# Pairwise tower on one core: the first twelve couples gathered one 128-sample block at a time, each four gathers followed by a wait for their landing, and product kinds read from a table

## What is computed

```python
e = jnp.stack([tbl_0[ids[:, 0]], ..., tbl_39[ids[:, 39]]], axis=1)      # 512 x 40 x 64
p, q = e[:, rowidx], e[:, colidx]                                       # all pairs i < j
z = jnp.einsum('bie,fie,bif->bi', p, param, q)                          # 512 x 780
h = jnp.concatenate([z, dense_ctx], axis=1)
h = jnp.maximum(h @ W_top1 + b_top1, 0.0)
h = jnp.maximum(h @ W_top2 + b_top2, 0.0)
y = h @ W_top3
```

## Time and profile before

| | |
|---|---|
| median of three runs | 346.36 us |
| lowest, highest | 344.58, 348.38 us |
| the profiled execution, its own time | 347.48 us |
| its span (first to last instruction) | 345.7 us |
| what lies around the span | 1.8 us |
| TensorE's granted clock, mean | 0.985 |
| busy: PE, DVE, ACT, GpSimd | 304.5, 260.8, 231.3, 217.4 us |

### The profile page before, as it was taken

One profiled execution on the slowest core, in us unless ns is written; L12 is line 12 of the kernel. 1 busy time (PEld: TensorE's weight loads), 2 busy tenths in 40 slices (PEclk: granted clock), 3 DMA queues, 4 the chain that ended last, 5 costly groups with the idle time before them and its releaser, 6 DMA issues.

```text
span 345.7 us, 7011 instructions
## 1 busy us (share of the span) xinstructions
PE 304.5 (88%) x2192; PEld 156.7 (45%) x2192; DVE 260.8 (75%) x278; ACT 231.3 (67%) x1783; POOL 217.4 (63%) x217
## 2 busy tenths in 40 slices
PE   0348837987999999999999999989999999999997
PEld 0123413443544444445654646554544534456665
DVE  0024773994999999999888697867789999986450
ACT  1000854675799779989835998893889988990003
POOL 5777777888688888888876867864686322220000
PEclk9999996998999999999999999999999999999999
DMA  3133584452444433411145453318433234000000
GB/s 78 27 77 94 147 288 147 150 144 94 126 139 141 154 95 95 156 33 35 25 121 139 133 159 99 123 47 322 143 126 123 58 123 149 2 1 3 0 2 0
DMA packets 12935, 35.57 MB, mean 103 GB/s; under 512 B 4705, under 2 KB 5985, under 8 KB 11618
## 3 DMA queue, kind: packets, MB, share of 16 engines
q1 hardware_dynamic: 7778, 29.88, 25.8%
q0 software_dynamic: 5120, 5.25, 7.5%
HBM read 35.12 MB, written 0.00 MB: 102 GB/s over the span
## 4 chain that ended last, share of the span: by engine, by line
PE 56%; issue 15%; DVE 14%; POOL 10%; ACT 3%; DMA 3%; DVEq 0%
PE upsum L596 18%; DVE prod L665 12%; PE upsum L591 11%; POOL emb L431 10%; PE zbank L546 9%; PE upsum L490 4%; PE abank L490 4%; PE abank L468 2%; ACT prod L703 2%; DMA emb<-tbl,rows_id 2%; PE upsum L558 2%; DVE z L639 2%; PE upsum L562 1%; PE abank L526 1%; PE upsum L615 1%
## 5 line engine op out<-in xcount | busy, mean ns | idle before, releaser
L703 ACT ACTIVATE prod<-prod 128x64 f32<-128x64 f32 x864 | 206.5, 243 | 7.2 <-DVE prod L665 6.5
L431 POOL DMA_INDIRECT emb<-tbl,rows_id x160 | 151.7, 948 | 52.0 <-issue 37.9
L703 ACT ACTIVATION_READ_ACCUMULATOR prod<-prod 128x1 f32 x864 | 163.7, 189 | 0.0
L665 DVE TENSOR_TENSOR prod<-upsum,emb 128x1024 f32<-128x1024 f32 x108 | 128.0, 1215 | 24.8 <-PE upsum L596 24.6
L596 PE MATMUL upsum<-w,xT 64*128 64x512 f32 x432 | 114.6, 630 | 3.6 <-DVE prod L665 2.6
L665 DVE TENSOR_TENSOR prod<-upsum,xT 128x1024 f32<-128x1024 f32 x72 | 85.7, 1215 | 24.2 <-PE upsum L591 24.1
L448 POOL TENSOR_TENSOR prod<-prod 128x512 f32<-128x512 f32 x51 | 65.0, 1277 | 38.8 <-DVE prod L665 38.2
L591 PE MATMUL upsum<-xT,w 64*128 64x256 f32 x576 | 78.4, 399 | 2.0 <-DVE prod L665 1.3
L591 PEld LDWEIGHTS upsum<-xT,w 64*128 64x128 f32 x576 | 54.8, 191 | 28.7 <-issue 13.6
L596 PEld LDWEIGHTS upsum<-w,xT 64*128 64x128 f32 x432 | 37.8, 189 | 48.0 <-issue 24.1
L546 PE MATMUL zbank<-prod,sel 128*32 128x256 f32 x696 | 50.8, 386 | 0.0
(11 more groups left out here) (42 smaller groups left out, 156.9 us busy)
## 6 DMA issues: line engine op xcount, KB each, us to landing
w<-W_top SPq DMA_DIRECT2D x2, 1792.0 KB, 9.4
emb<-tbl,rows_id POOLq DMA_INDIRECT x160, 2.5
w<-param SPq DMA_DIRECT2D x2, 1248.0 KB, 6.9
w<-param SPq DMA_DIRECT2D x2, 1152.0 KB, 5.0
w<-param SPq DMA_DIRECT2D x2, 1120.0 KB
w<-param SPq DMA_DIRECT2D x2, 1024.0 KB, 4.9
w<-param SPq DMA_DIRECT2D x2, 992.0 KB, 4.8
w<-param SPq DMA_DIRECT2D x2, 896.0 KB
```

The costliest lines, as they stand in the source:

```text
L431: pool.indirect_dma_start(emb[:, c, f, :], None, tables[f], bass.IndirectOffsetOnAxis(ap=rows_id[:, c, f:f + 1].bitcast(U32), axis=0),).th ...
L665: dve.tensor_tensor(to.rearrange("p (h q) -> p h q", h=2), t[:], f.broadcast_to([P, 2, BANK]), ALU.mult).then_inc(multiplied, 1)
L703: last = act.activation(ring[:, x * E:(x + 1) * E], ring[:, x * E:(x + 1) * E], ACT.Copy, accum_out=z_view(u)[:, x:x + 1])
```

## The change

The gathers of half 0's first twelve couples (0 to 11) are made block by block: first the 24 gathers of block 0, then the 24 of block 1. Ahead of every four of them but the first two fours, GpSimd waits until the four just issued have landed (a semaphore per couple for block 0, `first_gathered`). That makes ten waits. All later gathers keep their numbers: couple 12 at 16 and 18, couple 13 at 21 and 23.

The stretches of units get a part. Part 0: eleven units of block 0 of couples 4 to 11 come first, with a turn of block 0 alone ("xa", one transpose). Part 1: the other 25 units of couples 1 to 11, with the turn of block 1 ("xb"). Part 2 is the rest. The parameters of couples 4 to 11 are loaded twice, once for each part. The unit count stays 200, and unit 36 is still the first of couple 12.

The kinds are no longer made by shares but read from `KINDS`. Counted over both kernels:

| units | T | C | S | H | V |
|---|---|---|---|---|---|
| before, all 200 | 72 | 20 | 54 | 51 | 3 |
| after, all 200 | 72 | 20 | 52 | 34 | 22 |
| before, 0 to 29 | 9 | 5 | 8 | 5 | 3 |
| after, 0 to 29 | 6 | 5 | 6 | 0 | 13 |
| before, 36 to 99 | 24 | 4 | 18 | 18 | 0 |
| after, 36 to 99 | 30 | 4 | 17 | 13 | 0 |
| before, 100 to 199 | 36 | 10 | 27 | 27 | 0 |
| after, 100 to 199 | 34 | 10 | 27 | 20 | 9 |

```diff
-TURNS_BACK = [0, 0, 0, 0, 0, 0, 0, 0, 2, 2, 4, 4]
+TURNS_BACK = [1, 0, TURN_BACK]
-GATHER_FIRST, GATHER_FROM, GATHER_STEP = 10, 6, 5
+GATHER_FROM, GATHER_STEP = 16, 5
-SHARES = [(0, 0.55, 0.35, 0.1, 0.0), (14, 0.42, 0.33, 0.0, 0.25)]
+FIRST = 12
+KINDS = ["VVSV-VSVVVSV",
...
+    for n in range(4, FIRST):
+        stretch(0, n, 0)
+        for m in range(0, n - n % 2 - 3, 4):
+            by = next(kinds[0])
+            one_block[(n, m)] = by != "-"
+            if by != "-":
+                add(by, "SVH", s=0, n=n, m=m, c=0)
+        stretches[-1]["end"] = len(units)
...
-            def gather(s, f):
-                for c in range(s * PER, (s + 1) * PER):
-                    pool.indirect_dma_start(
...
-            for n in range(GATHER_FIRST):
-                gather(0, 2 * n)
-                gather(0, 2 * n + 1)
+            for c in range(PER):
+                for n in range(FIRST):
+                    if n % 2 == 0 and (c > 0 or n >= 4):
+
+                        for x in (n - 2, n - 1):
+                            if c == 0 or n == 0:
+                                pool.wait_ge(first_gathered[x % FIRST], 32)
+                            else:
+                                pool.wait_ge(gathered[0][x], 32)
+                    gather(0, 2 * n, c)
+                    gather(0, 2 * n + 1, c)
...
-            def turn_x(s, n, many):
+            def turn_x(what, s, n):
+                many = 2 if what == "xx" else 1
+                blocks = {"xa": [0], "xb": [1]}.get(what, range(PER))
                 for x in range(many):
-                    pe.wait_ge(gathered[s][n + x], 16 * 2 * PER)
+                    first = s == 0 and n + x < FIRST
+                    if first:
+                        pe.wait_ge(first_gathered[n + x], 32)
+                    if what != "xa":
+                        pe.wait_ge(gathered[s][n + x], 16 * 2 * (PER - 1 if first else PER))
```

## The result

The changed kernel takes 363.13 us (median of five executions), the kernel before 346.23 us in the same comparison. The recorded ratio is 1.043, 95% interval 1.038 to 1.049; the two medians alone give 1.049. It was forecast at 359.8 us, within 351 to 369. One of the five, a slow one, took 611.62 us and stands outside the ratio, and no trace shows why; the other four took 359.48 to 363.21 us, with a median of 362.6. The profiled execution, with a span of 357.7 us, is the shortest of them. So the trace explains 12.0 us of the 16.9 between the medians, and for the rest there is no trace.

A forecast was written before the change was run, and what follows sets the result against it. It took slow gathers to bound the start up to the double turn, and the engines the rest. +14.9 - 3 + 1.5 = +13.4 us on 347.48 gave 360.9, with the median 1.1 lower: 359.8 us, range 351 to 369.

The forecast's parts named there:

- The H additions that go: GpSimd's gather queue before the double turn: three H additions between gathers vanish, 1.16 us each, -3.5 us.
- The ten waits: GpSimd's gather queue: each undisturbed wait makes a step 2.72 us instead of 1.25, +14.7 us for ten.
- Disturbed landings: Gathers landing late at the start, one beside the 1792 KB load: +6 us for ten, between 0 and 14.6.
- The last landing: From the fifty-sixth gather's start to the double turn: 2.45 us instead of 4.7, -2.3 us.
- Double turn: TensorE's turn of couples 12 and 13, which needs 56 gathers: +14.9 us, coming at about 95 us.
- Couple 11's turn: Its second block, turned behind the double turn right ahead of its unit: 0.9 to 2.8 us, taken as +1.5.
- The rest: Engine work behind the double turn under the new kinds: -3 us, between -6 and +1.5.
- The other bound: Check by unit prices on units 36 to 99, with 3.3 us of the last 100 units: -8 us outermost.
- The signs: Trace after: some 20 us of pauses, couple 13's gather about 92 us, 253 to 256 us from double turn to last product.
- the first (early products pay, landings short): Rival: double turn only +7.4 us later, stretch behind it up to 8 us shorter; 346 us, chance 0.10.
- The waits do not bite: Rival at GpSimd's waits: four landings have come by the time the fourth is issued; -7.3 us, 339 us, chance 0.04.
- Landings get long throughout: Rival at the start: parameter loads press on the gathers, 14.6 us instead of 6, ScalarE delays the turn; 370 us, chance 0.10.

The follow-up runs named there:

- the run with waits one late: Changed kernel with its ten waits kept in place, each asking for the landing of the four gathers before the last four: 339.15 us, ratio 0.980 to the kernel before.
- the turns ahead: Changed kernel without its ten waits, part 1's block 1 turns two units ahead of their own units: 335.20 us, ratio 0.968 to the kernel before.

## Why the prediction was right

The direction and the place held, and so did the signs of the large terms: the waits stretch the gather chain, TensorE meets it at the double turn, and the table of kinds gives some back. The median lies 3.3 us above the forecast and in its range. The profiled execution's 359.48 us lies 1.4 us under the 360.9 worked out for it, and that closeness is luck: two errors offset each other.

- **The H additions that go, -3.5 us.** Held: without its 25.1 us of added pauses the fifty-sixth gather would start at 71.95, where pure issue gave 72.0. Between 88.31 and 97.05 all steps are 1.25 us, seven of them.
- **The ten waits, +14.7 us.** Mis-sized. An undisturbed step was 3.2 us, not 2.72; with a mean of 2.24 us for the six undisturbed pauses, ten make 10 x (2.24 - 0.30) = 19.4 us. The run with one semaphore shows that 2.72 was right for a wait on one (0.94 + 1.73 = 2.67), and that naming two costs the other half microsecond. The step that failed is "GpSimd needs some 0.27 us to start", taken from a wait on one semaphore; with two it was 3.2 - 2.45, some 0.75 us.
- **Disturbed landings, +6 us.** Held: the four long pauses exceed 2.24 by 0.27, 0.53, 1.22 and 3.73 us, 5.75 in all. The longest is the one beside the load of W_top1; moving that load took it away. What stretched the others is not shown.
- **The last landing, -2.3 us.** Held: 2.42 us.
- Double turn: forecast 95.15 (80.25 + 14.9), measured 99.47. The difference, 4.3 us, is that of the waits.
- **Couple 11's turn, +1.5 us.** Held in size: 12.55 against 11.32 us, +1.2. The granted clock was lower in this stretch too (0.75, before 0.85), and no run separates the two.
- **The rest, -3 us, between -6 and +1.5.** Mis-sized: -8.4 us in the traces (-8.7 to the last product), outside the term's own range. The step that failed is "of the 255.6 us to the last product only 5.9 us are without a matmul", used as a bound. Busy TensorE is no proof that TensorE is the limit. Its chain ran through VectorE, ScalarE and issue time for three tenths of half 1, and the new table turned most of that into TensorE's work. From the double turn to the last product, time without a matmul fell from 5.9 to 0.9 us (248.14 - 247.20) while the whole fell by 7.5 us; so some 2.5 us came out of time in which TensorE had counted as busy. The other bound, unit prices (-8), was just passed. In medians the kinds were worth 4.0 and 4.5 us.
- **The signs.** The pauses sum to 28.1 us where some 20 were forecast, and the fifty-sixth gather starts at 97.05 where 92 was. VectorE's first and eleventh product come at 24.08 and 53.19 (forecast 23 and 50). The stretch from the double turn to the last product, 248.14 us, lies outside the 253 to 256 given for it and only 0.14 us from the 248 under which the forecast called itself wrong.

Of the rivals, the first (early products pay, landings short) is half seen in the kernel without waits: it is under the kernel before, but through the kinds, and its double turn is 0.7 us later than before. "The waits do not bite" fell with the first pause; it is what the run with waits one late made true. "Landings get long throughout" did not come: six of ten pauses were undisturbed. The first rival's reason, that early products pay, no run shows on its own.

The Trainium skill (DMA: Bandwidth & Descriptors, section "Rules for kernel authors") asks to issue early and wait late; the pair of runs with waits on the last four and on the four before, 363.1 and 339.2 us, shows it on this kernel. Its statement that a DMA engine takes turns between queues packet by packet (section "Queues, rings and completion order") may hold here, but it did not protect a small gather: 5.97 us of pause beside a 1792 KB load, 2.54 without it.

## What to carry to other kernels

A wait in an issuing queue, right behind the transfers it asks for, cost 1.4 to 1.9 us at each undisturbed stop (a step of 2.67 or 3.2 instead of 1.25), and it delayed everything queued behind it; asked one group late, the same wait was free. When judging what a reordering may win, take the bound from the chain of waits and the prices of the units, not from an engine's busy share. And before work is moved to an engine that looks idle, look at what else stands in its queue: here ScalarE's copies were worth more than the V sums taken off VectorE.

## What the runs showed that was not expected

- A pause of GpSimd for one semaphore of gathers was 1.7 to 1.8 us where undisturbed, for two or three 2.1 to 2.3 us, with four gathers in flight in either case. A third semaphore that had long been met added nothing.
- A wait whose landing had already come cost nothing visible: the gap stayed 0.30 us.
- The kernel without waits ran between 334.5 and 341.6 us, a wider spread than the kernel before (343.7 to 347.9 in the same comparison); with the turns ahead it was 333.7 to 335.5. What makes the spread was not looked into.
